# LayerNorm of the attention's input on a turned copy of the tokens, statistics spread by memory, banks by name

## What is computed

```python
x = x + attention(layernorm(x), ctx, w_q, w_k, w_v, w_o, b_o)   # 16 heads of 64, per sequence of 128
x = x + experts(layernorm(x), gate, W1, b1, W2, b2)             # top 2 of 8 experts, 256 -> 512 -> 256
# layernorm(x) = (x - mean) / sqrt(var + 1e-5), without weights
```

## Time and profile before

| | |
|---|---|
| median of three executions | 1585.24 us |
| profiled execution, its time | 1586.61 us |
| its span on the core | 1584.8 us |
| TensorE busy | 1551.1 us, 98% of the span |
| VectorE busy | 1176.3 us, 74% |
| ScalarE busy | 1109.5 us, 70% |
| GpSimd busy | 817.8 us, 52% |
| DMA | 145.05 MB, mean 92 GB/s |

### The profile page before, as it was taken

The page is one execution under the profiler, slowest core; times in us unless marked ns, Lnnn a source line. Parts: engine busy times, 40 slices in busy tenths (PEclk is TensorE's granted clock), DMA queues, the critical chain, the costliest instruction groups (busy, mean ns, idle before and its releaser), DMA issues.

```text
span 1584.8 us, 45359 instructions
## 1 busy us (share of the span) xinstructions
PE 1551.1 (98%) x14116; PEld 1452.1 (92%) x14117; DVE 1176.3 (74%) x3796; ACT 1109.5 (70%) x3357; POOL 817.8 (52%) x946
## 2 busy tenths in 40 slices
PE   6999999999999999999999999999899999999997
PEld 5899989999989999999999999989799999999997
DVE  4677777777777777777777777776787777777775
ACT  4667767677777677776676776776766677777774
POOL 2345455454555455455455545455466555555556
PEclk9999999999999999999999999999999999999998
DMA  7422211122211122121122221111799755555554
GB/s 190 129 67 90 73 60 60 60 72 95 70 63 60 60 67 98 62 73 60 60 66 85 76 73 60 60 60 64 247 244 257 132 88 85 89 84 91 84 82 62
DMA packets 106443, 145.05 MB, mean 92 GB/s; under 512 B 12768, under 2 KB 88672, under 8 KB 106144
## 3 DMA queue, kind: packets, MB, share of 16 engines
q1 hardware_dynamic: 60944, 89.00, 18.1%
q0 software_dynamic: 26816, 37.32, 13.5%
q10 hardware_dynamic: 18640, 18.19, 4.4%
HBM read 77.09 MB, written 67.38 MB: 91 GB/s over the span
## 4 chain that ended last, share of the span: by engine, by line
issue 41%; PE 30%; POOL 20%; DVE 3%; DMA 2%; ACT 1%; POOLq 1%; DVEq 1%; SPq 0%; ACTq 0%
PE bank_a L1408 8%; POOL lists L666 7%; PE bank_t L1408 5%; PE bank_s L1408 5%; PE bank_v L1408 5%; POOL prob L673 4%; POOL rstd L652 2%; POOL stage_room L715 2%; POOL stage_room L711 2%; PE bank_a L1602 2%; DVE hid L1336 1%; PE bank_s L1426 1%; PE bank_v L1441 1%; DMA out<-stage_room,number 1%; PE bank_t L1415 1%
## 5 line engine op out<-in xcount | busy, mean ns | idle before, releaser
L673 POOL TENSOR_TENSOR prob<-prob,inv 128x512 f32<-128x512 f32 x256 | 270.9, 1058 | 528.5 <-DVE inv L960 527.8
L781 ACT ACTIVATE prob<-bank_s,low 128x128 f32<-128x128 f32 x1024 | 363.3, 376 | 41.8 <-DVE low L955 41.7
L739 POOL DMA_INDIRECT out<-stage_room,number x142 | 232.5, 1637 | 53.8 <-issue 53.5
L955 DVE TENSOR_REDUCE low<-bank_s 128x4 f32<-128x512 f32 x256 | 175.6, 686 | 98.4 <-PE bank_s L1426 98.3
L774 ACT ACTIVATE probt<-bank_t 128x512 f32<-128x512 f32 x256 | 153.4, 599 | 114.5 <-PE bank_t L1415 114.4
L781 ACT ACTIVATION_READ_ACCUMULATOR prob<-bank_s,low 128x1 f32 x1024 | 221.2, 216 | 0.0
L1054 DVE SCALAR_TENSOR_TENSOR stage_room<-xin,wo_t 128x256 f32<-128x256 f32 x480 | 179.0, 427 | 0.0
L889 ACT ACTIVATE hidt_h<-hid 128x512 fp32r<-128x512 f32 x142 | 89.6, 632 | 112.9 <-DVE hid L1336 111.2
L1415 PE MATMUL bank_t<-ident,prob 128*128 128x128 f32 x1024 | 161.4, 280 | 5.2 <-POOL prob L673 5.2
L1408 PE MATMUL bank_a<-xt_l,wq_h 128*128 128x256 f32 x512 | 153.5, 300 | 3.6 <-DVE xt_l L970 3.6
L811 ACT ACTIVATE ot_h<-bank_v 128x512 fp32r<-128x512 f32 x128 | 77.3, 604 | 113.3 <-PE bank_v L1441 113.3
(11 more groups left out here) (229 smaller groups left out, 4723.9 us busy)
## 6 DMA issues: line engine op xcount, KB each, us to landing
stage_room<-lists ACTq DMA_DIRECT2D x67, 265.0 KB, 3.0
halves<-stage_room SPq DMA_DIRECT2D x32, 512.0 KB, 4.2
homes<-halves SPq DMA_DIRECT2D x16, 1024.0 KB, 6.2
xin<-in_x SPq DMA_DIRECT2D x32, 256.0 KB, 2.8
stage_room<-in_x SPq DMA_DIRECT2D x32, 256.0 KB, 3.3
stage_room<-in_w SPq DMA_DIRECT2D x32, 256.0 KB, 4.3
out<-stage_room SPq DMA_DIRECT2D x32, 256.0 KB, 2.2
cin<-in_ctx SPq DMA_DIRECT2D x32, 128.0 KB, 2.6
```

Source lines behind the costliest of these rows:

```text
L673: pool.tensor_tensor(prob[:, n % 4, :, :], prob[:, n % 4, :, :], wide(inv[:, n % 4, :], P), ALU.mult).then_inc(s_norm.sem, 1)
L739: pool.indirect_dma_start(out, bass.IndirectOffsetOnAxis(ap=number[:, u, b:b + 1], axis=0), ysum[:, u, b, :], None, compute_op=ALU.add).th ...
L781: e = act.activation(prob[:, n % 4, h, :], bank_s[n % 2][:, h * P:(h + 1) * P], ACT.Exp, bias=low[:, n % 4, h:h + 1], scale=-1.0, accum_ou ...
L955: dve.tensor_reduce(low[:, n % 4, :], bank_s[n % 2][:, :].rearrange("p (h k) -> p h k", h=4), AX.X, ALU.min).then_inc(s_low.sem, 1)
```

## The change

The host gives the kernel a second copy of the tokens, `x_t`, with the 256 values along the rows (as it does already for the context). The kernel loads 256 columns of it into `xraw`, 128 partitions x 2 chunks x 256 tokens. As a partition now holds one value of all tokens, mean and inverse deviation of each token are needed on every partition: the 128 x 2 x 2 numbers are stored to `ln_rows` in memory and loaded from there into `ln_all`, all 512 of them on each partition. VectorE subtracts and multiplies with them in place, then the high and low parts are made from SBUF. The four transpositions and the event t0 are gone. With 15 events in place of 16, each event has a bank of its own in a table.

The core of the diff:

```diff
-        [("o1", FROM0), ("t0", NEXT)],
+        [("o1", FROM0)],
...
+    BANK_OF = {"q10": 0, "k10": 1, "o0": 2, "k11": 3, "q11": 0, "o1": 1, "v10": 2, "v11": 3,
+               "q00": 0, "k00": 1, "q01": 2, "k01": 3, "v00": 1, "f0": 0, "v01": 2}
...
+            def ln_through(engine, it):
+                if not isinstance(it, int) or it >= 0:
+                    engine.wait_ge(ln_in, (it + 1) * 16)
+                wait(engine, pool_step, it, "rstd1")
+                engine.dma_start(ln_rows, mean_var[:, 0, :, :]).then_inc(ln_out, 16)
+                engine.wait_ge(ln_out, (it + 2) * 16)
+                wait(engine, xn_step, it - 1, "xn")
+                engine.dma_start(ln_all.rearrange("p t b k -> p (t b k)"), ln_rows.rearrange("t b k -> (t b k)").rearrange(
+                    "(o n) -> o n", o=1).to_broadcast([P, 4 * P])).then_inc(ln_in, 16)
...  # SyncE, load_x: after xin, before cin
+                    sp.dma_start(xraw.rearrange("p c b t -> p c (b t)"),
+                                 x_t[:, cols].rearrange("(c p) t -> p c t", p=P)).then_inc(xt_in, 16)
...  # SyncE, body, before it waits for o1
                         load_x(it)
+                        ln_through(sp, it)
...  # GpSimd: the power goes beside the mean
-                    pool.tensor_tensor(rstd[:, k, :], shifted[:, k, :], mhalf[:, :],
+                    pool.tensor_tensor(mean_var[:, 0, :, 1] if k == 0 else rstd[:, k, :], shifted[:, k, :], mhalf[:, :],
...  # ScalarE, body, before exps(it, n); in the first pair ln_through runs here, at n = 1
+                        if n == 4 and has(it, NEXT):
+                            wait(act, a_full, it, "q11")
+                            wait(act, xn_step, it, "xn")
+                            act.activation(xt[0][:, 0:DC, :], xraw.rearrange("p c b t -> p c (b t)"),
+                                           ACT.Copy).then_inc(xa_hi.sem, 1)
...  # VectorE
+                def of_tokens(k):
+                    return ln_all[:, :, :, k].rearrange("p t b -> p b t").rearrange(
+                        "p (o b) t -> p o b t", o=1).to_broadcast([P, DC, 2, P])
+                def normalise_turned(it):
+                    dve.wait_ge(xt_in, (it + 2) * 16)
+                    dve.wait_ge(ln_in, (it + 2) * 16)
+                    dve.tensor_tensor(xraw[:, :, :, :], xraw[:, :, :, :], of_tokens(0), ALU.subtract).then_inc(xn_step.sem, 1)
+                    wait(dve, xn_step, it, "centred")
+                    dve.tensor_tensor(xraw[:, :, :, :], xraw[:, :, :, :], of_tokens(1), ALU.mult).then_inc(xn_step.sem, 1)
+                def low_of_tokens(it):
+                    wait(dve, xa_hi, it, "x")
+                    dve.tensor_tensor(xt[1][:, 0:DC, :], xraw.rearrange("p c b t -> p c (b t)"),
+                                      xt[0][:, 0:DC, :].bitcast(F32), ALU.subtract).then_inc(xa_lo.sem, 1)
...  # VectorE, body, n = 4: after the inverse of u3 and the joins, before v10
+                        if n == 4 and has(it, NEXT):
+                            low_of_tokens(it)
...  # VectorE, body, end of n = 1 and of n = 3 (there before the three x_scores)
-                        if n == 1 and has(it, NEXT):
-                            normalise(it, 0, xin, [xn[:, 0, :], xn[:, 1, :]])
+                        if n == 3 and has(it, NEXT):
+                            normalise_turned(it)
...  # TensorE, product
-                        for b in range(2):
-                            for c in range(DC):
-                                last = pe.transpose(dst[:, (2 * c + b) * P:(2 * c + b + 1) * P],
-                                                    xn[:, b, c * P:(c + 1) * P], ident[:, :])
+                        if name == "q00":
+                            wait(pe, xa_lo, it, "x")
```

More of the change, by code:

```diff
@@ L71, in wait, with program @@
         engine.wait_ge(signal.sem, value - back)
-def program(nc, x, ctx, w_q, w_k, w_v, w_o, w_ot, b_o, b_oc, gate, gate_t, w12, b1, b2, out):
+def program(nc, x, x_t, ctx, w_q, w_k, w_v, w_o, w_ot, b_o, b_oc, gate, gate_t, w12, b1, b2, out):
     tokens, D = x.shape
@@ L225, in program @@
             cin = place("cin", 2, 2 * P)
-            xn = place("xn", 2, D)
-            place("not_used", WORK + HOME - taken_to[0])
+            xraw = place("xraw", DC, 2, P)
+            ln_all = place("ln_all", P, 2, 2)
+            assert taken_to[0] == WORK + HOME
             qt = place("qt", 2, CHUNKS // 2, 2 * P)
@@ L361, in by_products, with a_bank @@
                 return isinstance(it, int) and it < 1
[L363 to L369, removed]
+            def a_bank(name):
+                return bank_a[BANK_OF[name]]
             def bank_before(it, name):
+                same = [n for n, _ in A_EVENTS if BANK_OF[n] == BANK_OF[name]]
                 if not isinstance(it, int):
[L374 to L378, removed]
+                    k = same.index(name) - 1
+                    return (it if k >= 0 else it - 1), same[k]
+                order = [(j, n) for j in range(-1, PAIRS + 1) for n in a_full.present(j) if n in same]
+                k = order.index((it, name)) - 1
                 return order[k] if k >= 0 else (it, None)
@@ L439, in program @@
             T_EARLY, T_ENDS, T_ALL = 23, 24, 48
-            bank_at = {name: a_bank(PAIRS, name) for name in ("o0", "o1", "f0")}
+            bank_at = {name: a_bank(name) for name in ("o0", "o1", "f0")}
             PLACES_AT = 5
             bank_h, bank_y = [bank_s, [bank_at["o0"], bank_at["o1"]]], [bank_t, bank_v]
-            bank_first = a_bank(PAIRS - 1, "v11")
+            bank_first = a_bank("v11")
             assert len({id(bank) for bank in (bank_first, *bank_at.values())}) == A_BANKS
@@ L509, in body @@
                         wait(sp, c_lo, it - 1, "c")
-                        wait(sp, ln1_step, it - 1, "ln1")
+                        wait(sp, xa_lo, it - 1, "x")
+                        wait(sp, ln1_step, it - 1, "bn1_1")
                         if not isinstance(it, int) or it > 1:
@@ L822, in body @@
                             numerators(it, x1[:, :, D:])
+                        if isinstance(it, int) and (it, n) == (-1, 1):
+                            ln_through(act, it)
+                        if n == 4 and has(it, NEXT):
[3 more added lines that the diff above has]
+                                           ACT.Copy).then_inc(xa_hi.sem, 1)
                         if has(it, CUR):
@@ L962, in second_part @@
                 def second_part(it, name):
-                    src = a_bank(it, name)
+                    src = a_bank(name)
                     kind, k = name[0], int(name[-1])
[L965 to L972, removed]
+                    wait(dve, a_full, it, name)
+                    if kind == "v":
                         last = dve.tensor_copy(vv[:, int(name[1]), k, :], src[:, :])
@@ L1039, in rows_of @@
                     dve.wait_ge(sent, (it - 1) * 64 + 16)
-                    normalise(it, 1, x1, [rows[:, b, 0:D] for b in range(2)])
+                    normalise(it, x1, [rows[:, b, 0:D] for b in range(2)])
                 def x_scores(it, first, many):
@@ L1446, in product @@
                 def product(it, name):
-                    dst = a_bank(it, name)
+                    dst = a_bank(name)
                     kind, k = name[0], int(name[-1])
@@ L1560, in body @@
                                 product(it, name)
-                                if isinstance(it, int) and it == -1 and name == "t0":
-                                    bias_scores()
+                        if isinstance(it, int) and (it, n) == (-1, 3):
+                            bias_scores()
                         if n in VALUES and has(it, VALUES[n][1]):
```

44 lines of the change are left out of this document (22 added, 22 removed).

## The result

| | before | changed |
|---|---|---|
| median of six executions | 1582.54 us | 1658.18 us (1648.43 to 1662.72) |
| ratio | | 1.0469, 95% interval 1.0452 to 1.0487 |
| profiled execution, its span | 1584.8 us | 1646.7 us |

The kernel is 4.7% slower. The time is within the range given, but the change is 76 us where 30 were forecast. The profiled execution is the fastest of the six; the other five took 1656 to 1663 us.

The account below looks back on a forecast made before the run. TensorE, busy 98% of the span, bounds the kernel. To 1586.6 us it added 30 x 0.92 = 27.6, less 0.4, plus 3 for the start: 1616.8, stated as 1616 us against the median; range 1597 to 1664.

Parts of the forecast that it names:

- The transpositions: On TensorE after o1: removing the four transpositions gives back 0.44 us an iteration, 14 us in 32 iterations.
- Place and chain: End of VectorE's n = 3: u3's inverse 1.05 us later, low part delays GpSimd, TensorE waits 1.36 us at u3.
- the plain price: VectorE's two new operations at n = 3: 0.69 us duration each, the strided SBUF source adding nothing.
- The round through memory in the loop, and the banks: Statistics stored and reloaded in 6.6 us of 11.2 available, hidden by 4.6 us; the changed bank predecessors cost nothing.
- The price of the step: 16-byte step in VectorE's two operations: taken as zero, bounded above by 0.53 us per operation.
- Its rival, 1647 us: Strided source halves the rate of VectorE's two operations: 1.98 us per iteration, clock kept; chance 0.24.
- The start: Before the first q00: statistics through a full DMA system, q00 near 17.6; 3 us taken, ends 1 and 10.
- The clock: TensorE's granted clock: taken as full, as it stayed after a wait of 1.40 us.
- the rival with the falling clock: Half rate, and TensorE's clock falls after each 2.4 us wait: 48 us on top, 1695 us; chance 0.07.
- The rival on the other side: VectorE does the two operations in its pause before o1, nothing late: 14 us gained, 1574 us; chance 0.07.

Follow-up runs that it names:

- the fastest kernel: Changed kernel with 8-byte step, first pair as before, low part before u4's lowest, two operations between u2's inverse and o1's addition: 1571.30 us, ratio 0.9923.
- the later low part: Changed kernel with the low part of the tokens at n = 4 moved behind v10 and ot_l: 1640.92 us, ratio 1.0374.
- the last kernel above: The 1571.30 us kernel's order, but statistics laid as in the changed kernel, with a step of 16 bytes: 1571.48 us, ratio 0.9932.

## Why the prediction was right or wrong

**The transpositions: right.** 0.44 us forecast, 0.47 scaled from leaving three out, 0.44 in the fastest kernel (34.16 to 33.72).

**Place and chain: right.** The two operations delay the inverse of u3, the low part lies beside GpSimd's multiplication with VectorE ahead, GpSimd takes 0.48 us longer, and TensorE waits there and nowhere else. With the plain price true (the step of 8 bytes) the iteration is 34.97 us where 35.08 was forecast. The 0.11 us between are about what GpSimd took less: the prediction gave it 1.66 us (530.06 to 531.72), and it took 1.52. In the trace this wait is 1.01 us of idle time, yet the iteration is 1.25 us longer than one without a wait (34.97 and 33.72), where 1.36 was forecast. A wait costs more than its idle time: TensorE's busy time is 33.97 us in the iteration with the wait and 33.72 in the one without (windows), 0.25 us more. Up to some 0.17 us of that, an estimate, is how idle time is counted: a matmul of 0.40 us is followed by the next one after 0.23 (525.51 and 525.74 in the changed kernel), and idle time begins only at its end.

**The round through memory in the loop, and the banks: right.** 1.50 us between the two issues, the statistics used at 522.36, 9.2 us after the load's issue at 513.17. It stays covered with pieces of 16 and of 8 bytes; a store of 512 pieces, 6.6 us longer, used the cover up.

**The price of the step: wrong.** The step that failed is the choice between the ends, zero and 0.53 us each. I took zero because the nearest row, a reduction of 32 elements read from a bank, "speaks for the plain price, weakly, as it is a bank". It is 0.40 us, three quarters of the way to the other end. This is 0.81 us an iteration, 24 us, the largest part of the error. It was of another memory and another operation, with few elements, so it could not bound the cost for a source in SBUF. The Trainium skill (SBUF — State Buffer, the note on SBUF "cachelines") asks for two hits in a line of 16 bytes. By that rule a float32 source with a step of 8 bytes is free and one with 16 is dear, and the trace agrees (0.69 and 1.09 us). The note gives no figure for VectorE. The prediction set the rule below a weaker row. Its rival, 1647 us, came nearest to the profiled execution at 1648.43, but by luck: it had 1.98 us an iteration where 1.62 was measured, and 2.6 us for the start and nothing for the clock, where these took 10 and 5.

**The start: wrong.** 3 us taken, 10 to 12 measured, at the upper end of 10 us named. The step that failed: "3 and 5 us for the two transfers". The store took 9.5 us in a DMA system that is full there, as the earlier trace rows had shown for another, and the load 7.6 (issued at 15.49, VectorE begins at 23.1). These 17.1 us, in place of 8.5 with the second issue, are nearly all of the 9.2 us by which q00 comes later than the 17.6 forecast. What is queued behind ln_through on ScalarE, the table and wq_h, was not counted either, but it is done before the load has landed.

**The clock: wrong.** The forecast had it full, as waits of 1.40 us in the earlier trace rows left it. At waits of 1.8 us it falls in some iterations, not in all as the rival with the falling clock had it: 5 to 6 us in the profiled execution, and about 10 more in the median of all six, by the mean clock of the others and by the 14 us of the later low part. This follows from the price of the step: with 0.40 us less twice the waits are 1.01 us, and the clock of those executions is 0.994 to 0.996.

In sum: 30 us were forecast; the step adds 24, the rest of the iteration takes 3 off (0.11 us each), the start adds 7 to 9 and the clock 14 to 15. These are 72 to 75 of the 76 us. That 1658 us lies in the range is partly luck: the range left out the fall of the clock, and its upper end came from other terms, the dear step and a dear start.

**The rival on the other side: right in its mechanism.** It was given 0.07 and 1574 us, "if VectorE could do the two operations in the pause before o1". With the two operations there alone the kernel took 1609 us, some 12 of them for the start. With the first pair as before, and the low part and x_scores moved as well, it took 1571; which of the two moves was needed wasn't measured apart.

## What to carry to other kernels

A step on TensorE's list removed at the price of work on a less busy engine is won or lost by where that work stands in the other engine's order: the same operations on VectorE cost the loop 49 us in one order (30 x 1.62) and left it 13 us faster than before in another (30 x 0.43). Look for the unit whose result TensorE takes with the least room (0.75 us here), put nothing ahead of its inputs, and move the new work into the pause before. And where a cost has two ends and no row of the same memory and size, weigh the dear end by what it would hit: here it lay on the tightest chain.

## What the runs showed of the hardware

- VectorE, 128x512 float32, both sources in SBUF, one read with a step: 0.69 us at 4 bytes (dense), 0.68 to 0.69 at 8, 1.09 at 16.
- A store of 512 float32 from 128 partitions, issue to the issue that waits for it: 1.50 us in 128 pieces of 16 bytes, 3.62 in 256 of 8, 8.11 in 512 of 4. In the first microseconds, with a DMA share of 1.03 from 6 to 15.5 us, 128 pieces took 9.5 us:

```profile
ln_rows<-mean_var ACTq DMA_DIRECT2D x1, 2.0 KB, 9.5
```

- Where VectorE's and GpSimd's operations on SBUF lie beside each other the later one takes longer (GpSimd 1.52 us in place of 1.04 beside one of 0.67), and with two in a row on VectorE both grow: 1.09 to 1.85 and 1.04 to 1.73 us. GpSimd's issue of an indirect DMA grows too, from 1.0 to 1.69 us.
- A wait of TensorE of 1.8 us was followed by a granted clock below full in four of the 31 iterations of the profiled execution and not in the others; with 1.34 us none was in the loop. Single waits of 2.18, 2.55 and 2.61 us (before, the two operations ahead of o1's addition, and the last kernel above) were followed by one, a single wait of 1.86 us was not.
